# Graphs staggered by three slots, a four of heads multiplied inside the next slot, ten of 16 heads turned through memory

## The reference

```python
for l in range(attn_w.shape[0]):                      # L0, three layers
    scores = si[:, :, None] + sj[:, None, :] + attn_b[l]
    scores = jnp.where(scores >= 0, scores, 0.2 * scores)
    attn = jax.nn.softmax(jnp.where(mask, scores, -jnp.inf), axis=-1)
    agg = jnp.einsum('bij,bjd->bid', attn, x)
    h = layernorm(x + agg, g1[l], beta1[l])
    ff = jax.nn.gelu(h @ W1[l] + b1[l], approximate=False) @ W2[l] + b2[l]
    x = layernorm(h + ff, g2[l], beta2[l])
...
scores = a_src[:, :, :, None] + a_dst[:, :, None, :] + b_att[None, :, None, None]   # L1, eight heads
scores = jnp.where(mask, jax.nn.leaky_relu(scores, negative_slope=NEG_SLOPE), NEG_INF)
out = jax.nn.relu(jnp.einsum('bhij,bhjk->bhik', jax.nn.softmax(scores, axis=-1), xh))
...
x = _layernorm(x + _L0_gnn_ref(...), axis=-1)
x = _layernorm(x + _L1_gnn_ref(...), axis=-1)
```

## Time and profile before

| | |
|---|---|
| median of 3 runs | 2322.04 us (2321.35 to 2323.39) |
| the profiled execution | 2323.47 us |
| its span in the trace | 2321.7 us, so 1.8 us lie around it |
| PE busy | 2213.5 us, 95% |
| DVE busy | 1809.9 us, 78% |
| ACT busy | 1684.1 us, 73% |
| TensorE clock granted, mean | 0.985 |

### The profile page before, as it was taken

One profiled execution on the slowest core, in us unless ns is written; L12 is line 12 of the kernel. 1 busy time (PEld: TensorE's weight loads), 2 busy tenths in 40 slices (PEclk: granted clock), 3 DMA queues, 4 the chain that ended last, 5 costly groups with the idle time before them and its releaser, 6 DMA issues.

```text
span 2321.7 us, 32320 instructions
## 1 busy us (share of the span) xinstructions
PE 2213.5 (95%) x10501; PEld 1560.0 (67%) x10501; DVE 1809.9 (78%) x5722; ACT 1684.1 (73%) x3243; POOL 201.1 (9%) x200
## 2 busy tenths in 40 slices
PE   3999999999999999999999999999999999999976
PEld 2676767766776677677677667766776776777643
DVE  5457587779788787887788787887878878766778
ACT  2433468776778778787787777787778877888796
POOL 0010110000100010001100001000010011001100
PEclk9999999999999999999999999999999999999978
DMA  6011024343163232532443421632316323200111
GB/s 219 11 37 55 10 96 135 93 150 101 46 197 109 76 127 54 188 105 63 133 130 103 153 90 58 188 104 89 124 47 199 97 65 104 69 19 19 37 42 37
DMA packets 115874, 219.30 MB, mean 94 GB/s; under 512 B 7768, under 2 KB 57212, under 8 KB 110332
## 3 DMA queue, kind: packets, MB, share of 16 engines
q1 hardware_dynamic: 115708, 217.24, 29.8%
HBM read 164.52 MB, written 52.69 MB: 94 GB/s over the span
## 4 chain that ended last, share of the span: by engine, by line
PE 75%; DVE 16%; ACT 5%; issue 3%; POOL 1%; DMA 0%; SPq 0%; DVEq 0%; POOLq 0%; ACTq 0%
PE ffn L1240 21%; PE av L1157 14%; PE ffn L1229 11%; PE av L1229 11%; PE pT L1140 8%; PE av L1181 4%; DVE prob L777 2%; DVE prob L768 2%; PE av L1216 2%; ACT xs L555 1%; DVE lone L729 1%; POOL rstd L469 1%; PE trow L1119 1%; DVE xs L903 1%; DVE stats L716 1%
## 5 line engine op out<-in xcount | busy, mean ns | idle before, releaser
L1240 PE MATMUL ffn<-w_sb,G 128*128 128x256 f32 x3072 | 741.1, 381 | 0.0
L1240 PEld LDWEIGHTS ffn<-w_sb,G 128*128 128x128 f32 x3072 | 561.3, 191 | 90.3 <-issue 24.3
L777 DVE CUSTOM_DVE_ANT_0 prob<-trow,mask 128x512 f32<-128x512 f32 x676 | 439.3, 686 | 34.3 <-PE trow L1119 19.4
L1229 PE MATMUL ffn<-hT,w_sb 128*128 128x512 f32 x768 | 355.0, 595 | 1.1 <-ACT hT L534 1.1
L1140 PEld LDWEIGHTS pT<-ident,prob 128*128 128x128 f32 x2032 | 255.9, 143 | 148.0 <-issue 101.6
L1229 PE MATMUL av<-hT,w_sb 128*128 128x512 f32 x768 | 353.5, 593 | 0.0
L469 POOL TENSOR_TENSOR rstd<-veps,mhalf 128x4 f32<-128x4 f32 x127 | 167.2, 1317 | 2082.9 <-DVE veps L712 2082.9
L515 ACT ACTIVATE prob<-prob,s 128x512 f32<-128x512 f32 x484 | 331.5, 716 | 2.4 <-DVE nm L784 1.8
L1140 PE MATMUL pT<-ident,prob 128*128 128x128 f32 x2032 | 312.1, 278 | 20.0 <-DVE prob L840 7.6
L521 ACT ACTIVATE prob<-prob,nm 128x512 f32<-128x512 f32 x448 | 317.7, 712 | 0.0
L1157 PE MATMUL av<-xs,prob 128*128 128x257 f32 x1024 | 244.3, 380 | 3.9 <-ACT prob L526 3.9
(11 more groups left out here) (154 smaller groups left out, 2727.2 us busy)
## 6 DMA issues: line engine op xcount, KB each, us to landing
w_sb<-in_L_gnn_W SPq DMA_DIRECT2D x48, 1024.0 KB, 8.4
blocks_dram<-blocks SPq DMA_DIRECT2D x168, 256.0 KB, 4.2
prob<-blocks_dram SPq DMA_DIRECT2D x42, 1024.0 KB, 4.8
trow<-rows_dram SPq DMA_DIRECT2D x127, 256.0 KB, 3.2
adj_sb<-in_adj SPq DMA_DIRECT2D x16, 1024.0 KB, 7.0
xin<-in_x SPq DMA_DIRECT2D x16, 512.0 KB, 6.3
x0r<-in_x SPq DMA_DIRECT2D x16, 512.0 KB, 5.8
out<-o SPq DMA_DIRECT2D x15, 512.0 KB, 3.3
```

What stands on the lines that cost most here:

```text
L777: return v.tensor_tensor_reduce(out=out_[:, t, :], in0=targets, in1=mask[:, t, :], scale=1.0, scalar=LEAST, op0=ALU.add, op1=ALU.max, accu ...
L1229: last = te.matmul(ff1[f % len(ff1)][:], w1_sb[:, g // 2 % STAGES, dt, f * P:(f + 1) * P], hT[:, dt, :], start=dt == 0, stop=dt == DT - 1)
L1240: last = te.matmul(ffn[part][:, at:at + D], G[:, f, t * P:(t + 1) * P], w2_sb[:, g // 2 % STAGES, f, :], start=f == 0, stop=f == FT - 1)
```

## The change

**Order of the units.** The graphs no longer go in pairs. From slot 5 on, three slots in a row hold layer 2 of one graph, layer 1 of the next and layer 0 of the one after, so a graph ends its first network in each third slot (`unit_of`, `begun`). There is one empty place near the end (`BUBBLE`), as the last graph has no partner for its last two layers. Weights are loaded for each slot.

**Heads.** A finished graph's eight heads are made in three slots, three, two and three (`MADE_IN_SLOT`). In what follows, and in the prediction, the three kinds of slot have letters:

- **A** (g % 3 = 2): heads 5, 6 and 7 of a graph are turned; the four 0 to 3 is multiplied; `keep_masks`.
- **B** (g % 3 = 0): heads 0, 1 and 2 of the next graph are turned; the four 4 to 7 is multiplied, and the graph of that four ends (`graph_sum`, `graph_out`); `make_masks`.
- **C** (g % 3 = 1): heads 3 and 4 are turned; no four; the next graph leaves the first network (`begun`).

**Moved heads.** Heads 1, 2, 4, 6 and 7 of each graph from 1 to 12 are moved (and heads 1 and 2 of graph 13), 62 instead of 42; heads 0, 3 and 5 are turned by PE, so that PE turns one head in a slot. `turned_ahead`, which put some block transposes ahead of the attention, is gone: the first moved head of a slot is transposed behind the attention, the second at the slot's end.

**The four.** It is multiplied in the slot after the one in which its last head is turned, behind the fourth first product (f = 3), with `heads_back` behind the sixth; the row of targets goes ahead of the sixth instead of the seventh. Two pieces of the second product less stand ahead of the attention, one more inside it.

**The end.** Eight heads instead of 16 belong to the graph that ends last; 13 heads instead of 17 are turned behind the last unit.

```diff
-BY_BLOCKS = (1, 2, 4, 5, 8, 10, 13)
-AHEAD = (2, 4)
...
+MADE_IN_SLOT = {2: 3, 0: 2, 1: 3}
+FIRST_MADE = {LAYERS * 2: HEADS // 2, LAYERS * 2 + 1: HEADS // 2}
+BY_BLOCKS = (1, 2, 4, 6, 7)
...
 def unit_of(u):
-    return u // SLOTS, u % SLOTS % 2, u % SLOTS // 2
+    if u < len(FIRST_SLOTS):
+        return FIRST_SLOTS[u]
+    return [(u // 3 - 1, 2), (u // 3, 1), (u // 3 + 1, 0)][u % 3]
...
 def moved(q):
-    return q < LAST_HEADS - 2 * HEADS and q % (2 * HEADS) in BY_BLOCKS
+    return q < LAST_HEADS - 2 * HEADS + 3 and q % HEADS in BY_BLOCKS and q >= HEADS
...
+def spent_at(g):
+    return side_by_side(turned(g - 1))[1] if g else None
```

On DVE (the loop over slots):

```diff
+                if four is not None:
+                    heads_out(four)
                 for q in new[:1]:
                     head_maxima(q)
...
-                for q in turned_ahead(g):
-                    turn_blocks(q)
-                attention(s2, l2, *new[1:2])
+                attention(graph2, l2, *new[1:2])
                 for q in turned_behind(g)[:1]:
                     turn_blocks(q)
-                if done is not None and done % 2 == 0:
+                if done is not None:
                     graph_sum(done)
...
+                elif g > 3 and g % 3 == 2:
+                    keep_masks(g // 3 % 2)
+                elif g > 3 and g % 3 == 0 and g // 3 + 1 < GRAPHS:
+                    make_masks((g // 3 + 1) % 2)
                 for q in new[2:]:
                     head_made(q)
                 for q in turned_behind(g)[1:]:
                     turn_blocks(q)
```

On PE (the loop over slots):

```diff
+                ahead, inside, behind = (4, (1, 1), (1, 1, 1, 1)) if four is None else (2, (2, 1), (2, 1, 2, 1))
...
                 for f in range(FT):
-                    if f == FT - 2:
+                    if f == (FT - 2 if four is None else FT - 3):
                         first_target_row()
                     first_product(g, f)
+                    if f == 3 and four is not None:
+                        attend_heads(four)
+                    if f == 5 and four is not None:
+                        heads_back(four)
                     if f >= T:
                         for q in heads[:1]:
                             turn(q, f - T)
```

More of the change, by code:

```diff
@@ L1065, in _ @@
                     turn_blocks(q)
-                fed_forward(s, 1)
-            layer_ends(0, LAYERS - 1)
+                fed_forward(graph, 1)
+            first, second, third = made(REGULAR)
+            layer_ends(GRAPHS - 2, LAYERS - 1)
             first_network_ends(GRAPHS - 2)
-            times_gain(1, LAYERS - 1)
-            heads_out(LAST_HEADS - 2 * SIDE)
-            head_made(LAST_HEADS - 1)
-            plus_bias(1, LAYERS - 1)
+            times_gain(GRAPHS - 1, 1)
+            head_made(first)
@@ new lines, in _ @@
+            plus_bias(GRAPHS - 1, 1)
+            head_made(second)
+            for t in range(T):
+                turned_out(first - 1, t)
+            fed_forward(GRAPHS - 1, 0)
+            head_made(third)
+            for t in range(T):
+                turned_out(first, t)
+            fed_forward(GRAPHS - 1, 1)
+            layer_ends(GRAPHS - 1, 1)
+            dve.wait_ge(s_hn, c("hn"))
+            dve.sem_inc(s_passed, 1)
+            scores(GRAPHS - 1, LAYERS - 1)
+            heads_out(first - 5)
@@ new lines, in _ @@
+            first_targets(1)
+            graph_begins(GRAPHS - 2)
+            for t in range(T):
+                head_targets(third + 1, t)
+                if t < T // 2:
+                    first_exponents(2 * t)
+                    first_exponents(2 * t + 1)
+            head_maxima(third + 1)
+            attention(GRAPHS - 1, LAYERS - 1, third + 2)
+            heads_out(first - 1)
+            graph_sum(GRAPHS - 3)
+            head_made(third + 3)
+            times_gain(GRAPHS - 1, LAYERS - 1)
@@ L1074, in _ @@
+            plus_bias(GRAPHS - 1, LAYERS - 1)
+            graph_out()
+            head_made(third + 4)
+            for t in range(T):
+                turned_out(third + 1, t)
+            for t in range(T):
+                turned_out(third + 2, t)
+            fed_forward(GRAPHS - 1, 0)
+            head_made(third + 5)
             keep_masks(1)
+            head_made(third + 6)
             for t in range(T):
-                turned_out(LAST_HEADS - 3, t)
-            graph_begins(GRAPHS - 2)
@@ L1167, in attend_heads @@
             def attend_heads(q):
-                by_act, by_vector = all_out[q + SIDE - 1, T - 1]
+                by_act, by_vector = all_out[[h for h in range(q, q + SIDE) if not moved(h)][-1], T - 1]
                 pe.wait_ge(s_prob, by_act)
@@ L1315, in _ @@
                             turn(q, f - T)
-                for t in range(T):
-                    piece(t)
-                attention(s2, l2, g + 1, lambda i: piece(4 + i))
-                if place == 0:
-                    attend_heads(four)
+                pieces(ahead)
+                attention(graph2, l2, g + 1, lambda i: pieces(inside[i]))
                 for t in range(T):
@@ L1326, in _ @@
                         state_in(begin, t - T + DT)
-                    piece(6 + t)
-                if place == 0:
-                    heads_back(four)
+                    pieces(behind[t])
                 for t in range(T):
-                    for q in heads[2:3]:
+                    for q in heads[2:]:
                         if not moved(q):
```

541 lines of the change are left out of this document (273 added, 268 removed).

## The result

The changed kernel takes 2575.8 us (median of 4 runs, 2575.2 to 2577.4) against 2322.3 us (4 runs of the kernel before on the same chip): 1.109 times the time before, 95% interval 1.107 to 1.111. It is slower by 253 us. The forecast was 2530 us, with a range of 2400 to 2605; the time lies 6 us above the narrower 2490 to 2570, which was given a chance of 70%.

What follows compares the result with a forecast made beforehand. PE was taken to set the pace, 135.75 us a graph. Work of 131.4 plus waits of 19.3 gave 150.7, twelve times; with start to 487.6, tail 205 and clock 30, the forecast was 2530 us, range 2400 to 2605.

Steps and rivals of the forecast that it cites:

- the narrower 2490 to 2570: The forecast's own range around 2530 us for the whole kernel, chance 70%.
- All five places of waits: PE waits per graph: B's f=3 1.4, B's four 8.3, C's f=0 3.0, f=3 4.1, row of targets 2.5 us.
- The clock: Behind B's 8.3 us wait, PE's clock falls: 2.5 us a graph, bounds 0 to 3.5, 30 us in all.
- the 131.4 of its work: Time of a graph in A, B and C if PE never waited: 131.4 us, 4.35 less than before the change.
- in C nothing, as PE waits for DVE anyway: Clock cost in C taken as nothing, bounds 0 to 3.5 us.
- with waits as in C: Slot 7, which turns four heads while a graph leaves: 57 us, 7 of them waits.
- without waits: Slot 9 is a B without waits, 43.5 us, ending at 487.6.
- filled by three heads' work on ACT: Slot without partner near the end, its bare chain filled by ACT; tail from slot 46 taken as 205 us, bounds 190 to 230.
- The chain that lies bare: In the slot without partner: 30 us from DVE's start to the fourth attend's end, some 10 more to the next first product.
- PE sets the pace after all: Rival: DVE and head 7 are in time, nothing of the 19.3 us is left, 2269 us; chance 4%.
- Only one of the two delays: Rival: head 7 lands in time in B, only DVE's lateness counts, 2401 us; chance 8%.
- More clock lost: Rival: C's waits cost clock too, B's the upper bound, 2585 us; slower landings up to 1.4 each, 17; chance 16%.

Runs made afterwards that it cites:

- The run with the graph's end moved: Changed kernel with the graph's end in B (sum, statistics, output) put behind the feed-forward's first half instead of ahead of it: 2574.9 us, ratio 1.108.
- the run with three moved heads: Changed kernel with only heads 1, 4 and 6 of each eight moved, 2 and 7 turned by PE: 2438.0 us, ratio 1.049.
- The run with two banks: Changed kernel with the second head's tiles in slots 7 and 8 turned in the order 1, 0, 3, 2: 2566.8 us, ratio 1.105.
- the runs with four: Changed kernel with head 7 of each graph turned by PE in A instead of moved: 2454.3 us, ratio 1.057.

## Why the prediction was right

**The direction and its mechanism.** DVE's part behind the fourth attend was put at 5.8 us late in A and 11.6 in B; the trace has 5.9 and 11.5 (part 1 of B starts at 663.5, and PE's pieces end at 652.0). All five places of waits were the foretold ones.

**The waits and the clock: the same time, split otherwise.** In the order of the sum (B's f=3, B's four, C's f=0, f=3, row of targets) the forecast has 1.4, 8.3, 3.0, 4.1 and 2.5 us, 19.3 in all; the rows have 1.4, 8.2, 3.1, 2.0 and 0.5, 15.3. (From the forecast's own terms the first two are 1.3 and 8.4; the sum is the same.) The clock was put at 2.5 us per graph, all in B, and nothing in C. By the windows it took 5.6, of which 2.3 in B and 3.3 in C; another 1.3 us of PE's 138.3 busy us lie above the 131.4 of its work without being the clock's. So 131.4 + 15.3 + 5.6 + 1.3 = 153.6, against 153.2 foretold with the clock.

That the two sums agree is not all luck. The forecast's reason for the zero, "in C nothing, as PE waits for DVE anyway", holds for the time and not for the waits: the deadline is DVE's, so a PE at half clock comes later and waits less. C's last two waits were 4.0 us shorter than forecast, and in their place came the 3.3 of the clock and 0.7 of other busy time. The run with the graph's end moved has other waits and the same time, too. But it holds narrowly, and that part is luck: 0.5 us was left at the row of targets, and in the run with three moved heads the half clock fell behind C's last wait, where nothing hid it, and cost 1.7 us. The Trainium skill (TensorE: Matmul & The Clock Gate, "Why this matters for your kernels") warns of idle gaps between bursts of matmuls. The trace agrees, behind C's waits of 3.1 and 2.0 us too: 655.1 to 658.5 and 665.4 to 668.7 at 0.50.

**The terms that were too small.** The forecast was 46 us low, and 43 of these lie in the span (2574.4 against 2531): 14 at the start, 5 in the rhythm (1843.2 measured, 1838.4 with the clock foretold) and 25 in the tail.

- Slots 6 to 9 were to end at 487.6 us and end at 501.6: 14 us. The step is "with waits as in C". Slots 7 and 8, where four heads are turned, took 6 and 5 more than the 57 and 50 of the sum. The run with two banks shows them at 58.0 and 51.3: two heads turned in one loop use one PSUM bank, which the sum did not count. Slot 9, foretold "without waits", is 3.4 us longer, 3.1 of it the wait at the next f=0.
- The tail was put at 205 us, within 190 to 230, and takes 229.6. The step is the slot without partner, "filled by three heads' work on ACT". Slot 46 with the empty slot takes 82.7 us; before, slot 46 alone took 47.0, a window whose columns are as above:

```profile
2111.30:2158.30 47.00, 47.00 (x241) 33.08 (x240) 34.98 (x116) 40.54 (x80) 5.75 (x4) 1.00 0.07 23
```

So the empty slot cost 35.7 us, where the sum's terms leave some 21 for it (from 210.4 less 5.3 for one head and 21 for four, up to 205). The chain that lies bare there took 43.5 us, from slot 46's last piece (to 2384.0) to the next first product, where 40 were foretold, and it was not filled: ACT stands idle for 31 of the 82.7 us. The last unit and what follows take 146.9 us against 163.4 before (210.4 less 47.0), so the fewer heads gave back 16.5 us where the sum has 26. What holds these last 147 us, with no engine busy for more than 108 of them, stays open; the loads of ACT's table are a small part.

**The rivals.** That PE sets the pace after all is refuted by the runs with four and with three moved heads, each with more PE work and each faster. Busy shares pointed the other way: PE had the highest, its work per graph fell from 134.5 us to 131.4, and the engine with 72% set the time of the one with 88%. The Trainium skill (Perfetto Trace Analysis, "Identifying the Most-Contended Engine") has the engine with the highest occupancy optimised first, but says "for Tensor judge headroom by MFU / LDWEIGHTS busy %". PE's weight loads (PEld) were busy for 67% before, DVE for 78%; MFU, the share of the peak arithmetic rate, stands in no row here. By these two shares DVE was the more contended, and the trace agrees.

"Only one of the two delays" fell too: the wait for head 7 and those for DVE are both in the rows. "More clock lost" was half right: C lost clock, but nearly all of that came off its waits, and B's 2.3 us were as forecast. Head 7's landing was not slowed: its read back took 4.8 to 4.9 us, as in the earlier trace rows, in eleven of the twelve graphs and 5.7 in one. The 1.4 us that were priced for it stand in no run.

## What to carry to other kernels

Where engines work in order and hand over at fixed places, ask for each handover who comes last and by how much; here an engine busy for 72% of the time stood behind all five waits, behind one of them through a DMA that it started late. Work that is moved ahead on the busiest engine shortens the cover that its partner had behind it: here the same change with DVE's work moved out of that stretch, and one head more turned by PE, was 225 us faster. Before a wait is taken away, look for the next one on the same engine, since a wait may only hide another, and price the start, the drain and any empty slot of a staggered schedule as stages of their own.

## What the runs showed of the hardware

Behind waits of 3.1 and 2.0 us in one slot, PE was granted half its clock for 3.4 and 3.3 us; behind waits of 1.4, 1.5 and 2.2 us in one slot it was in some graphs and not in others (the run with three moved heads). PE's wait for a landed DMA is shown without a releaser; in all twelve graphs PE started 0.09 us after the recorded landing, and in eleven of them SP's issue row plus the median time to landing gives that time to within 0.1 us. Turning a 512x512 head of float32 through memory took 13.1 us, from the start of the block transpose at 599.82 to the landing: 2.3 for the transpose, 6.0 until its four writes had landed and the read back was issued, 4.8 for the read back. Two tiles transposed one after the other into one PSUM bank cost PE 0.77 us of waiting for the copy between them, when nothing else delayed ACT's copy.
